# A Flamingo block on one core: six halved context tiles, their low halves made by VectorE, and another order at the start and in the last batch

## What is computed

```python
def _layernorm(x, axis=-1, eps=1e-05): ...
def _L0_xattn_ref(query, key):           # query (8,100,2048), key (8,722,2048)
    a = jnp.einsum('bqd,bkd->bqk', query, key)
    e = jax.nn.softmax(a, axis=-1)
    return jnp.einsum('bqk,bkd->bqd', e, key)
def _L0_ffn_ref(x, qweight, weight_scale, weight_zero_point, bias):
    w = _dequantize(qweight, weight_scale, weight_zero_point)   # 6-bit values, (2048, 2048)
    return jnp.einsum('bsk,nk->bsn', x, w) + bias
x = x + jnp.tanh(g_xattn[0]) * _L0_xattn_ref(_layernorm(x), ctx_4096)
x = x + jnp.tanh(g_ffn[0]) * _L0_ffn_ref(_layernorm(x), qweight, ...)
```

## Time and profile before

| | |
|---|---|
| Three runs | 596.57 (median), 585.42, 600.55 us |
| The profiled execution | 585.18 us, span 583.3 us |
| Busy: TensorE, VectorE, ScalarE, GpSimd | 98%, 62%, 49%, 37% |
| A steady batch | 45.7 us |
| Granted TensorE clock, mean | 0.999 |

### The profile page before, as it was taken

How to read it: one execution, slowest core, us unless ns; L and a number is a source line. 1 busy time by engine, 2 the same in 40 slices (tenths; PEclk the granted TensorE clock), 3 DMA queues, 4 the chain that set the end, 5 groups by cost and what they waited for, 6 DMA issues and landing times.

```text
span 583.3 us, 8789 instructions
## 1 busy us (share of the span) xinstructions
PE 569.0 (98%) x3454; PEld 409.8 (70%) x3454; DVE 358.9 (62%) x684; ACT 287.7 (49%) x451; POOL 217.0 (37%) x196
## 2 busy tenths in 40 slices
PE   7979999999999999999999999989999999999997
PEld 6969969968968968978977986555564444444445
DVE  6667717827836836745755764694859764654443
ACT  3756566568567666676675757354232220210000
POOL 3037177169259349439439519711000000000000
PEclk9999999999999999999999999999999999999999
DMA  8999649236947848738848668669756984872311
GB/s 247 296 299 242 193 160 319 66 104 225 228 144 249 225 108 298 224 98 261 265 104 281 193 161 366 225 111 284 233 183 187 252 237 134 194 152 66 89 55 40
DMA packets 44436, 113.69 MB, mean 195 GB/s; under 512 B 21027, under 2 KB 21283, under 8 KB 35779
## 3 DMA queue, kind: packets, MB, share of 16 engines
q1 hardware_dynamic: 27168, 107.71, 60.7%
q10 hardware_dynamic: 16970, 5.42, 5.2%
q0 software_dynamic: 256, 0.00, 0.0%
HBM read 89.26 MB, written 19.66 MB: 187 GB/s over the span
## 4 chain that ended last, share of the span: by engine, by line
PE 79%; DVE 7%; DMA 5%; POOL 3%; SPq 3%; issue 1%; ACT 1%
PE S L1164 18%; PE S L1056 12%; PE T L1010 8%; PE pv L1164 8%; PE S L1058 7%; PE pv L1094 6%; PE S L1094 6%; PE pv L1010 5%; POOL vlo L495 3%; DMA xa<-in_x 3%; DVE xres L783 3%; PE pv L1105 2%; PE S L1105 2%; DMA raw<-in_L_ffn_qweight 2%; SPq L330 2%
## 5 line engine op out<-in xcount | busy, mean ns | idle before, releaser
L495 POOL TENSOR_TENSOR vlo<-raw,vhi 128x2048 fp32r<-128x2048 f32 (+1 forms) x38 | 174.1, 4606 | 50.3 <-ACT vhi L563 50.3
L1056 PE MATMUL S<-khi,qT 128*100 128x362 f32 x512 | 141.3, 357 | 0.0
L1058 PE MATMUL S<-klo,qT 128*100 128x362 f32 x256 | 85.3, 333 | 3.5 <-DVE klo L912 3.0
L912 DVE TENSOR_TENSOR klo<-pv,khi 128x361 fp32r<-128x361 f32 x128 | 65.3, 527 | 23.6 <-ACT khi L552 23.0
L912 DVE TENSOR_TENSOR klo<-T,khi 128x361 fp32r<-128x361 f32 x128 | 65.7, 529 | 21.5 <-ACT khi L552 20.6
L563 ACT ACTIVATE vhi<-raw 128x2048 fp32r<-128x2048 f32 (+1 forms) x38 | 72.0, 1911 | 6.3 <-PE S L1094 6.2
L552 ACT ACTIVATE khi<-T 128x361 fp32r<-128x361 f32 x128 | 58.4, 475 | 33.0 <-PE T L1010 32.8
L1164 PE MATMUL S<-raw 128*128 128x512 f16 x320 | 71.7, 379 | 1.6 <-issue 1.6
L552 ACT ACTIVATE khi<-pv 128x361 fp32r<-128x361 f32 x128 | 58.6, 476 | 29.8 <-PE pv L1010 29.8
L1056 PEld LDWEIGHTS S<-khi,qT 128*100 128x100 f32 x512 | 67.9, 167 | 0.0
L1010 PE MATMUL T<-ident,raw 128*128 128x128 f32 (+1 forms) x416 | 64.0, 268 | 0.4 <-DVE qT L902 0.3
(11 more groups left out here) (128 smaller groups left out, 748.6 us busy)
## 6 DMA issues: line engine op xcount, KB each, us to landing
raw<-in_ctx SPq DMA_DIRECT2D x24, 1024.0 KB, 10.4
raw<-in_L_ffn_qweight SPq DMA_DIRECT2D x16, 768.0 KB, 7.7
raw<-in_ctx SPq DMA_DIRECT2D x12, 840.0 KB, 9.0
raw<-in_ctx SPq DMA_DIRECT2D x32, 256.0 KB, 10.2
xres<-in_x SPq DMA_DIRECT2D x8, 800.0 KB
x_scratch<-xres SPq DMA_DIRECT2D x8, 800.0 KB
rows_scratch<-xres SPq DMA_DIRECT2D x8, 800.0 KB
late<-x_scratch SPq DMA_DIRECT2D x24, 256.0 KB, 4.8
```

The costliest lines, as they stand in the source:

```text
L495: pool.tensor_tensor(vlo[0:r, k, :], raw[0:r, b % 2, t, :], vhi[0:r, k, :].bitcast(F32), ALU.subtract).then_inc(s_vlo, 1)
L912: dve.tensor_tensor(klo[:, slot, 0:GW], T[k][:, 0:GW], khi[:, slot, 0:GW].bitcast(F32), ALU.subtract).then_inc(s_free[k], 1)
L1056: pe.matmul(into[0:R, g, 0:MW], qT[:, h, c, :], khi[:, slot, :], start=(c == 0 and h == 0), stop=False)
L1058: last = pe.matmul(into[0:R, g, 0:MW], qT[:, 0, c, :], klo[:, slot, :], start=False, stop=(c == CH - 1))
```

## The change

All six tiles of batches 0 to 6 are halved (`HALVED = 6`), tile 5 last. VectorE makes the low halves of batches 0 to 6, each in two pieces of 1024 columns: tiles 3, 4, 5 and tile 0 of the next batch in the attend phase, tiles 1 and 2 (in batch 0 also 0) as hooks in the scores. GpSimd makes only the three of batch 7. ln1_norm moves from the attend phase into the scores, in front of step 30 (31 at i = 0); context_hi(i,2) moves from step 6 to step 2, the statistics of x from 17 to 15 (from 22 to 19 at i = 0). ln2_stats is cut in two. At the start SP waits for the first quarter of x before it loads context, ScalarE issues the second x in its step 4, and three quarters of queries(1) are turned inside scores(0). In batch 6 probs(7) is turned between the two parts of normed(0); batch 7 begins with float32 tile 3, and its two kinds of tiles alternate, each with a turning in front.

```diff
@@ -38,11 +38,11 @@
-    HALVED = 5
+    HALVED = 6
     PAIRS = 3
-    ORDER = [0, 1, 2, 5, 3, 4]
-
-    LAST_ORDER = [0, 1, 5, 3, 2, 4]
+    ORDER = [0, 1, 2, 3, 4, 5]
+
+    LAST_ORDER = [3, 0, 5, 1, 4, 2]
@@ -172,7 +172,6 @@
         s_coef = sem("s_coef")
-        s_pvt = sem("s_pvt")
         s_pv = sem("s_pv")
@@ -231,8 +230,9 @@
             elif i < LAST:
-                fill("x", 0, 4)
+                fill("x", 0, 2)
                 fill("P", LAST, 2)
+                fill("x", 0, 2, 2)
         for n in range(2):
@@ -291,12 +291,9 @@
-                if t < halved(b):
-                    lo_made(sp, b, t)
-                    if b == 0:
-                        sp.wait_ge(s_scores, 1)
-                else:
-                    sp.wait_ge(s_pvt, b + 1)
+                lo_made(sp, b, t)
+                if b == 0:
+                    sp.wait_ge(s_scores, 1)
@@ -330,8 +327,9 @@
+
+            sp.wait_ge(s_xa0[0], 16)
             context_pieces(0)
-            next_x(1)
             for k, g in enumerate((g_xattn, g_ffn)):
@@ -487,12 +485,13 @@
-            def context_lo(b, t):
+            def context_lo(t):
                 r = ROWS[t]
-                pool.wait_ge(s_vhi, b * HALVED + t + 1)
-                k = (b * HALVED + t) % PAIRS
-                pool.tensor_tensor(vlo[0:r, k, :], raw[0:r, b % 2, t, :], vhi[0:r, k, :].bitcast(F32),
+                pool.wait_ge(s_vhi, LAST * HALVED + t + 1)
+                pool.wait_ge(s_vlo, LAST * HALVED + t)
+                k = (LAST * HALVED + t) % PAIRS
+                pool.tensor_tensor(vlo[0:r, k, :], raw[0:r, LAST % 2, t, :], vhi[0:r, k, :].bitcast(F32),
                                    ALU.subtract).then_inc(s_vlo, 1)
@@ -508,21 +507,14 @@
             rstd(0, 1)
-            pool.wait_ge(s_q, NCH + 1)
-            for t in range(PAIRS):
-                context_lo(0, t)
             for i in range(B):
...
                     rstd(0, i + 2)
+                if i >= 1:
+                    rstd(1, i - 1)
                 if i == LAST - 1:
-                    rstd(1, i - 1)
-                for t in range(PAIRS, halved(i)):
-                    context_lo(i, t)
-                if i >= 1 and i != LAST - 1:
-                    rstd(1, i - 1)
-                if i < LAST:
                     for t in range(PAIRS):
-                        context_lo(i + 1, t)
+                        context_lo(t)
                 if i >= 1:
@@ -595,11 +587,11 @@
                 act.wait_ge(s_turned[k], u + 1)
-                if b >= 1:
+                if 1 <= b < LAST:
                     act.wait_ge(s_pv, b * NCH)
...
                 if b < LAST:
-                    act.activation(pT[0:ROWS[5], :], T[k][0:ROWS[5], 2 * R:3 * R], ACT.Copy)
+                    act.activation(ph[0:ROWS[5], 0, 5, :], T[k][0:ROWS[5], 2 * R:3 * R], ACT.Copy)
                     act.activation(ph[:, 0, 3:5, :], src, ACT.Copy).then_inc(s_phi, 1)
@@ -655,7 +647,11 @@
             queries(0)
-            keys_hi(0, {17: lambda: context_hi(0, 0), 22: lambda: context_hi(0, 1), 27: lambda: context_hi(0, 2)})
+
+            def second_x():
+                act.dma_start(xa[0:R, :], x[1]).then_inc(s_xa, 16)
+
+            keys_hi(0, {4: second_x, 17: lambda: context_hi(0, 0), 22: lambda: context_hi(0, 1), 27: lambda: context_hi(0, 2)})
             queries(1)
@@ -670,26 +666,28 @@
                 if i >= 1:
-                    between[6] = lambda: context_hi(i, 2)
+                    between[2] = lambda: context_hi(i, 2)
                 if i >= 2:
                     between[12] = lambda: ln2_norm(i - 2)
+                if i + 2 < B:
+                    between[30 if i else 31] = lambda: ln1_norm(i + 2)
                 keys_hi(i + 1, between)
...
                 exps(i + 1)
+                for t in range(PAIRS, HALVED):
+                    context_hi(i, t)
                 if i + 2 < B:
-                    ln1_norm(i + 2)
-                context_hi(i, 3)
-                context_hi(i, 4)
-                context_hi(i + 1, 0)
-                if i + 2 < B:
-                    queries(i + 2)
+                    queries(i + 2, (0, 1))
+                    context_hi(i + 1, 0)
+                    queries(i + 2, (2, 3))
                 else:
+                    context_hi(i + 1, 0)
                     lo_made(act, i, 3)
                     rows_hi(0, 0)
+                    probs(LAST)
+                    ln2_norm(i - 1)
                     rows_hi(0, 1)
-                    ln2_norm(i - 1)
                 context_hi(i + 1, 1)
-            probs(LAST)
             context_hi(LAST, 2)
@@ -783,11 +781,20 @@
-            def ln2_stats(i):
+            def ln2_stats(i, pieces=range(NCH)):
                 dve.wait_ge(s_x1, i * NCH + NCH)
-                for c in range(NCH):
+                for c in pieces:
                     stats_piece(1, i, xres[i % 2], c)
-                mean_and_variance(1, i)
+                if NCH - 1 in pieces:
+                    mean_and_variance(1, i)
+
+            def context_lo(b, t, half):
+
+                r, k, cols = ROWS[t], (b * HALVED + t) % PAIRS, slice(half * D // 2, (half + 1) * D // 2)
+                dve.wait_ge(s_vhi, b * HALVED + t + 1)
+                low = dve.tensor_tensor(vlo[0:r, k, cols], raw[0:r, b % 2, t, cols], vhi[0:r, k, cols].bitcast(F32), ALU.subtract)
+                if half:
+                    low.then_inc(s_vlo, 1)
@@ -803,7 +810,9 @@
                 dve.tensor_tensor(ph[:, 1, 3:5, :], T[k][:, 0:2 * R].rearrange("p (t r) -> p t r", r=R),
-                                  ph[:, 0, 3:5, :].bitcast(F32), ALU.subtract).then_inc(s_free[k], 1)
+                                  ph[:, 0, 3:5, :].bitcast(F32), ALU.subtract)
+                dve.tensor_tensor(ph[0:ROWS[5], 1, 5, :], T[k][0:ROWS[5], 2 * R:3 * R], ph[0:ROWS[5], 0, 5, :].bitcast(F32),
+                                  ALU.subtract).then_inc(s_free[k], 1)
@@ -926,38 +935,51 @@
             queries_lo(0)
-            hooks = pieces_of(1, 22, 2)
-            hooks[30] = lambda: centred(1)
+            hooks = pieces_of(1, 17, 3)
+            hooks[28] = lambda: centred(1)
             keys_lo(0, hooks)
...
                 if i + 2 < B:
-                    hooks = pieces_of(i + 2, 17 if i else 22, 3 if i else 2)
+                    hooks = pieces_of(i + 2, 15 if i else 19, 3 if i else 2)
                 else:
                     hooks = {16 + (15 * n + 3 * k) // 2: lambda n=n, k=k: unpack_piece(n, k) for n in range(2) for k in range(5)}
+                for n, (t, half) in enumerate([(t, half) for t in range(0 if i == 0 else 1, PAIRS) for half in range(2)]):
+                    hooks[5 + (5 * n + 1) // 2 if i else 5 + 2 * n] = lambda t=t, half=half: context_lo(i, t, half)
                 if i == 0:
-                    hooks[3] = lambda: row_max(0)
-                    hooks[13] = first_coef
+                    hooks[4] = lambda: row_max(0)
+                    hooks[18] = first_coef
                 keys_lo(i + 1, hooks)
...
                 if i >= 1:
-                    ln2_stats(i - 1)
+                    ln2_stats(i - 1, (0, 1))
+                for half in range(2):
+                    context_lo(i, 3, half)
+                if i >= 1:
+                    ln2_stats(i - 1, (2, 3))
+                for half in range(2):
+                    context_lo(i, 4, half)
                 coef(i + 1)
+                for half in range(2):
+                    context_lo(i, 5, half)
                 if i + 2 < B:
-                    queries_lo(i + 2)
+                    queries_lo(i + 2, (0, 1))
+                    for half in range(2):
+                        context_lo(i + 1, 0, half)
+                    queries_lo(i + 2, (2, 3))
             rows_lo(0, 0)
+            probs_lo(LAST)
             rows_lo(0, 1)
             residual(LAST - 1)
-            probs_lo(LAST)
             ln2_stats(LAST - 1)
...
             rows_lo(1, 0)
+            unpack(3)
             rows_lo(1, 1)
             scale_and_bias()
-            unpack(3)
             unpack(RT)
@@ -1102,12 +1124,12 @@
                         for n in range(NCH):
+                            if first:
+                                pe.wait_ge(s_x1, (b - 1) * NCH + n + 1)
                             last = pe.matmul(pv[n][0:R, :], p, raw[0:r, b % 2, t, n * 512:(n + 1) * 512],
-                                             start=False, stop=final)
+                                             start=first, stop=final)
                             if final:
                                 last.then_inc(s_pv, 1)
-                        if t == 5:
-                            last.then_inc(s_pvt, 1)
@@ -1193,17 +1215,16 @@
             pe.wait_ge(s_pad, 2)
-            scores(0)
-            queries(1)
+            scores(0, {2 * CH: lambda: queries(1, (0, 1)), 2 * CH + 2: lambda: queries(1, (2,))})
+            queries(1, (3,))
             for i in range(LAST):
...
```

(7 more changed lines are left out.)

## The result

The changed kernel is slower by 5%: its four runs have a median of 616.67 us (614.24 to 620.02), four of the kernel before 592.03; the ratio is 1.053, with a 95% interval of 1.045 to 1.060. Ratios here leave out the executions that lie more than 1.5% above the fastest of their own kernel (596.57 and 600.55 of before); medians do not. The forecast was 590.8 with a range of 577 to 601. The profiled execution took 614.24, its span is 612.1, 28.8 more than before.

The account below looks back on a forecast made before the run. TensorE, busy 98% of the span, was taken as the bound, any new hole costing in full. Terms +2.6 + 4.0 + 0.2 + 0.8 + 2.85 - 4.4 - 0.4 = +5.6 on 583.3 gave 588.9, plus 1.9: 590.8 us; range 577 to 601.

Parts of the forecast that it names:

- (5): Start: second x issued earlier, queries(1) inside the scores, first x quarter before context; -4.4 us, bounds -5 and +1.
- (6): End, attend(6) to the first multiply: less TensorE work but a 3.3 to 3.5 us hole before probs(LAST); -0.4 us.
- the zero taken for the tail: From the first multiply to the end: the 193.4 us stay untouched, 0 us.
- C: Rival, slower: a VectorE piece costs what it lasts, at 1.22 us total +13.5, time 598.7; chance 0.19.
- (1): Attend phase: tile 5 halved, 3.43 becomes 2.75, -0.68 us of TensorE per batch, seven times.
- (2): Attend phase: VectorE's chain makes the next first klo matmul late, losing 0.44 us; six times, +2.6.
- VectorE over 90% busy in a steady batch: Sign that the forecast is right: VectorE's busy share in a steady batch, with vlo pieces starting 1.13 us apart.
- (3): Scores: VectorE's pieces and ln1_norm open holes; 1.0 us each for i = 2 to 5, +0.2 at 1, +0.8 at 6.
- (4): Scores at i = 0: six pieces two steps apart and ln1_norm before step 31 open holes; +2.85 us.
- context after 11: Sign that the forecast is wrong: at the start, context landing after 11 us.
- D: Rival on TensorE's clock: the longer hole of the end lowers it to 1.2 GHz, +3 us; chance 0.52 shared with forecast and E.

Follow-up runs that it names:

- a7: Changed kernel, but GpSimd makes the low halves of tiles 1 and 2, so VectorE has no pieces in the scores (two in batch 0): 617.5 us.
- b1: Kernel before with only the changed kernel's start (SyncE waits for x, ScalarE issues the second x, its transposes inside the scores): 589.2 us.
- a4: Changed kernel without SyncE's wait for the first quarter of x; second x stays on ScalarE's queue: 611.3 us.
- a6: Changed kernel, SyncE storing rows(5) ahead of loading the second x tile, and x1(6) ahead of loading xres(7): 625.0 us.
- b3: Kernel before with 64 unused bytes behind ph, moving later buffers: median 587.7 us, ratio 1.0015.
- b2: Kernel before with 800 unused bytes behind ph, placing late as in the changed kernel: median 587.0 us, ratio 1.0005.
- a2: Changed kernel with the old order of the last two batches and the first x fills copied before vhi of (7, 0): 602.5 us.
- a3: Changed kernel with the whole start as before (SyncE's order, second x, centring, queries(1)): 611.3 us.
- mix: Changed kernel, VectorE making low halves of tiles 3 and 5 only, GpSimd the rest; start and last order mostly as before: 600.5 us, 1.026 of before.
- mix2: As mix plus a pad, VectorE making low halves of tiles 3, 4, 5 while GpSimd has none, GpSimd 0, 1, 2: 583.5 us, 0.992 of before.

## Why the prediction was wrong, step by step

Three steps failed: (5), (6) and the zero taken for the tail. They make 21.0 of the 23.2 us by which the span missed the sum; the time of 614.2 lies above every rival, C's 598.7 too.

(1) and (2) right: attend 0.55 shorter (expected 0.68), the first klo matmul 0.53 later (expected 0.44). The piece costs 1.14 (taken: 1.13), so C is out. The rule that the prediction takes from the Trainium skill, page "VectorE: DVE Perf Modes", section "The DRAIN you can't avoid", would put the starts 1.21 apart; the measured 1.14 is against it here. The same section adds that an instruction which is not held starts earlier, without a figure, and that fits. The sign "VectorE over 90% busy in a steady batch" did not come: it is 86%, 40.37 of 47.1.

(3) right for the middle batches, with (2) 1.49 to 1.58 against 1.44, and a7 shows the share of the pieces in the scores to be 0.74. For the last scores it missed 1.6: the text says of the context loads that none is late by more than 1 us, and did not follow the same `used` in front of the second load of weights. That load went out 1.0 us later into the scores than before and landed after 9.1 us instead of 5.2, which left VectorE waiting 2.77.

(4) right in size: 2.8 against 2.85. No run takes its pieces away cleanly; in a7 they are fewer and scores(1) is still no shorter.

(5) failed, by 5.3. It took a wait for one transfer (x, 3.18) as a loss that goes when its issue is moved. The first 0.8 came (the turning of x starts at 8.28 instead of 9.11), and the wait for x went; in its place TensorE waited 4.8 for context. The DMA engines are full from 10 us on, and what x gains the context gives: b1 and the sixteen starts show it, a4 shows that SyncE's wait alone is not the reason. "Should land just before TensorE asks" was the step, and the wrong sign it named (context after 11) came.

(6) failed, by 10.5. Its hole was right: 3.30 against 3.3 to 3.5. Missing were the slow clock behind it (D, held to be worth 3 and given no weight in the sum), 1.7 us there (4.1 for the tile behind it instead of 2.9, 0.5 for the turning) and 2.7 behind the second hole, and SyncE's queue, of which the text followed only the context loads: the later turning of x rows holds up a load of rows, the store of rows(5), the load of xres(7) and the store of x1(6), and through the last of them ScalarE: 5.8. a6 shows it.

"The 193.4 us behind the multiply are untouched" failed, by 5.2 in this execution, by up to 21 in relatives. The tail is not a fixed piece of TensorE work: it takes 193 us when the turned weights are in time and up to 214 when they are not; in the changed kernel TensorE waits 4.4 for them. With the old order of the last batches it was 192.8 to 193.7 in six of seven profiled executions, with the new one 194.3 to 214.2 in nine. The seventh, b3 with 198.3, waited 3.2 for turned rows instead, so 5 us of a single tail can be chance; the nine are not. What stays open is why. From 28 to 66 us behind the multiply the issues of stores, loads and turnings stand within 1.6 us of the same distance from it in before and changed kernel; but a turning lands 7.0 to 8.3 us (median of eight) after its issue in before, b1, b2 and b3, 9.7 to 10.8 in a2, a3, mix and mix2, and 12.3 to 14.3 in the rest. From 66 to 86 us behind the multiply everything is late, not the turnings alone: the windows view (455.86 to 475.86 before, 479.47 to 499.47 after) has the DMA engines of both kernels full (share 1.05 and 1.15), yet the changed one moves fewer bytes (281 and 189 GB/s). In this stretch the four kernels with five halved tiles move 265 to 281 GB/s, the twelve with six 180 to 235. The place of the buffers is not it. No cause was found, neither for the six halved tiles nor for the new order on top.

So most of the miss lies in the stretches of which only the engines were worked out and not the transfers: -4.8 was booked for start, last batches and tail, which brought +16.2; the +10.5 of steps (2) to (4) came as +12.6.

## What to carry to other kernels

When an order is changed, follow every queue that holds a wait for the moved work, to its last entry, and what waits for these: here one late turning of rows delayed a store, an in-place normalization behind it and, 30 us on, TensorE. A wait for a transfer in a stretch where the DMA engines are full is not a gain to be had by issuing it earlier. Divide subtractions of two SBUF operands between VectorE and GpSimd by time, not by amount, so that the two never run them together: between mix and mix2 this was worth 0.8 us a batch and 8.6 from attend(6) to the multiply.

## What the runs showed of the hardware

VectorE's subtraction of two SBUF operands and GpSimd's exclude each other: two pieces of 1.21 took 10.61 beside GpSimd's 9.10 and ended 2.21 behind it, and in mix2 GpSimd's steps of rstd, else 0.2 to 0.6 us, took 1.05 to 1.41 beside VectorE's pieces. The earlier trace rows had shown a milder case (5.73 for three; 1.34 alone). Not all of VectorE is held: in mix, beside GpSimd's subtraction at 168.76, two BATCH_NORM_STATS2, with one SBUF operand, took 1.28 as always, and klo, with one operand in PSUM, 0.52 in a7. The Trainium skill says this ("SBUF — State Buffer", "Who interferes with whom"): VectorE and GpSimd share a pair of ports, and this pair is an exclusive lock; a VectorE instruction with two SBUF inputs contends for it with a GpSimd one that reads SBUF, one with at most one SBUF input, outside the two-port modes, does not. These rows agree. The changed kernel avoids it by keeping GpSimd's subtractions out of batches 0 to 6, mix2 by giving them different times.

A hole of 3.3 us lowered TensorE's granted clock to 0.79 over 8 us, one of 5.8 to 0.67 over 10; those of 0.9 and 0.5 in each batch left it at 1.00. Between them the length alone does not tell: one of 1.89 at the start of before left it at 1.00, one of 1.83 at the start of mix lowered it to 0.80 over 5 us.

The kernel before, run over 50 times, took 584.5 to 605.3 us: a single run cannot show 2%.
